# Two attention stages of one kernel: where the causal mask is added, and which PSUM banks hold the scores

## The reference

```
# layer 0, cut to what matters (x: 16 x 256 x 256)
q, k, v = rope(x1 @ w_qkv.T + b_qkv)          # x1: x after a cross attention with a side input
scores  = q @ k.T / sqrt(16)                  # 16 heads of 16 channels, 256 x 256 per head
scores  = where(causal, scores, -inf)
out     = softmax(scores) @ v @ w_out.T + b_out
x = x + out;  x = x + fp4_ffn(category_linear(x))

# layer 1
du      = reaction_diffusion(x)
q, k, v = rope(rms_norm(du) * g @ W_qkv)      # 16 heads of 64 channels
q, k, v = cut into two segments of 128 tokens each
k, v    = 16 memory keys / values put in front: 144 keys per segment
scores  = where((j < 16) | (j - 16 <= i), q @ k.T / 8, -1e30)
x = x + softmax(scores) @ v @ W_out;  x = x + mixture_of_experts(mlp(x))
```

## Time and profile before

| | before |
|---|---|
| median of three runs | 2669.96 us |
| the profiled execution, its span | 2665.8 us, 2664.1 us |
| PE busy | 2463.0 us (92%) |
| PEld busy | 2191.2 us (82%) |
| DVE busy | 1836.6 us (69%) |
| ACT busy | 1229.0 us (46%) |
| POOL busy | 939.4 us (35%) |
| mean granted TensorE clock | 0.957 of full |

### The profile page before, as it was taken

One profiled execution on the slowest core, in us unless ns is written; L12 is line 12 of the kernel. 1 busy time (PEld: TensorE's weight loads), 2 busy tenths in 40 slices (PEclk: granted clock), 3 DMA queues, 4 the chain that ended last, 5 costly groups with the idle time before them and its releaser, 6 DMA issues.

```text
span 2664.1 us, 55131 instructions
## 1 busy us (share of the span) xinstructions
PE 2463.0 (92%) x19904; PEld 2191.2 (82%) x19904; DVE 1836.6 (69%) x3887; ACT 1229.0 (46%) x3774; POOL 939.4 (35%) x1016
## 2 busy tenths in 40 slices
PE   4799999999998559999999999979999999999999
PEld 3578778778877447888888888769999999999999
DVE  5666766766766556656666656447876988888877
ACT  2455555555555124554545454433333565555522
POOL 4332432333332324444544444402332222222054
PEclk7899999999998779999999999989999999999999
DMA  3221121111111032222112221122113677777534
GB/s 112 88 54 33 43 54 33 43 47 41 43 23 28 0 108 47 48 52 51 43 44 51 52 48 44 46 53 72 41 41 110 223 231 233 228 240 229 183 98 129
DMA packets 153077, 225.74 MB, mean 85 GB/s; under 512 B 54294, under 2 KB 123174, under 8 KB 142054
## 3 DMA queue, kind: packets, MB, share of 16 engines
q1 hardware_dynamic: 143942, 203.56, 26.7%
q0 software_dynamic: 8864, 18.66, 2.7%
HBM read 159.32 MB, written 27.16 MB: 70 GB/s over the span
## 4 chain that ended last, share of the span: by engine, by line
PE 75%; DVE 10%; ACT 7%; issue 4%; DMA 1%; POOL 1%; SPq 0%; another core or an unknown queue 0%; ACTq 0%; POOLq 0%; DVEq 0%
PE bank L55 56%; PE bank L140 6%; PE bank L1155 3%; ACT P L1336 2%; PE bank L1193 2%; PE bank L319 2%; PE bank L315 2%; PE bank L344 1%; PE bank L1150 1%; DVE qm L826 1%; PE bank L308 1%; DVE qr L833 1%; ACT L1384 1%; PE bank L1188 1%; ACT PTh L604 1%
## 5 line engine op out<-in xcount | busy, mean ns | idle before, releaser
L1336 ACT ACTIVATE P<-bank,mx 128x144 f32<-128x144 f32 x512 | 188.3, 380 | 373.0 <-DVE mx L1434 373.0
L1021 POOL TENSOR_TENSOR xe<-xe 128x704 f32<-128x704 f32 (+3 forms) x64 | 86.5, 1351 | 501.2 <-DVE xe L846 499.9
L55 PE MATMUL bank<-xD_hi,w1e_lo 128*128 128x256 f32 x880 | 254.2, 289 | 0.0
L55 PE MATMUL bank<-xD_hi,w1e_hi 128*128 128x256 f32 x880 | 249.4, 283 | 0.0
L55 PE MATMUL bank<-xD_lo,w1e_hi 128*128 128x256 f32 x880 | 249.3, 283 | 0.0
L55 PE MATMUL bank<-w2e_hi,hrD_lo 128*128 128x256 f32 x880 | 249.0, 283 | 0.0
L55 PE MATMUL bank<-w2e_lo,hrD_hi 128*128 128x256 f32 x880 | 249.0, 283 | 0.0
L55 PE MATMUL bank<-w2e_hi,hrD_hi 128*128 128x256 f32 x880 | 249.0, 283 | 0.0
L592 ACT ACTIVATE Ph<-bank,mx 128x128 f32<-128x128 f32 x256 | 93.9, 367 | 322.1 <-DVE mx L738 278.3
L2358 POOL DMA_INDIRECT xE<-d_y,ixs x78 | 110.9, 1422 | 343.4 <-PE bank L140 316.4
L1991 ACT ACTIVATE hD<-bank,b1E 128x256 f32<-128x256 f32 x312 | 128.6, 473 | 199.2 <-PE bank L55 191.8
(11 more groups left out here) (320 smaller groups left out, 7994.6 us busy)
## 6 DMA issues: line engine op xcount, KB each, us to landing
w1raw<-in_ew SPq DMA_DIRECT2D x39, 1024.0 KB, 5.8
w2raw<-in_ew SPq DMA_DIRECT2D x39, 1024.0 KB, 5.0
K<-Kn SPq DMA_DIRECT2D x256, 72.0 KB, 2.1
d_ys<-oE SPq DMA_DIRECT2D x39, 256.0 KB, 2.4
d_rot<-QK SPq DMA_DIRECT2D x16, 512.0 KB, 4.0
Rs<-d_rot SPq DMA_DIRECT2D x64, 128.0 KB, 4.3
Q<-Qn SPq DMA_DIRECT2D x128, 64.0 KB, 2.0
later<-Qn SPq DMA_DIRECT2D x128, 64.0 KB, 2.0
```

The source lines that it names most:

```text
L55: inst = e.matmul(out, l, r, start=k == 0, stop=k == len(pairs) - 1)
L1021: e.tensor_tensor(x, x, s, ALU.add).then_inc(*po.up())
L1336: inst = e.activation(P1[t % 2][:, n, :], bank[:, 144 * sg:144 * sg + 144], ACT.Exp, bias=mx1[t % 2][:, 2 * g + sg:2 * g + sg + 1], scale=1.0,
```

## The change

There are four edits.

1. The mask products on PE go, with `identb`. The mask is now added by DVE inside the pass that takes the maximum: `tensor_tensor_reduce` writes -(score + mask) to `Ph` (stage c: `P1`) in SBUF, and its accumulator gives the minimum of that, which is the negated maximum. Each such call is two instructions on DVE, one that streams and one that writes the accumulator out. There are four calls in a step of either stage; in stage c they take the place of two instructions.
2. ACT computes the exponential in place in SBUF, with scale -1.
3. Scores always use banks 0 and 1, turned weights banks 2 and 3. `scores(P+1)` therefore waits for `maxima(P)` (`v_mx`), and the wait for the copies of the pair before (`c_PT`) moves to `turn_heads`. In stage ab the three score blocks of a head become two products, of 128 and 256 columns.
4. In step 1 of stage ab ACT runs `spread_copy(b-1)` ahead of `exps(P+1)`, no longer behind it.

```diff
         def mask(n):
-            return maskb[:, 144 - n:144].rearrange("p (o n) -> p o n", o=1).broadcast_to((128, 2, n))
+            return maskb[:, 256 - n:256]
...
             # pe_ab, scores(P)
-                bank = [banks[2 * (P % 2) + g] for g in range(2)]
-                for g in range(2):
-                    if P >= 2:
-                        e.wait_ge(c_PT, 2 * P - 3 + g)
-                    e.matmul(bank[g][:, 0:384].rearrange("p (a n) -> p a n", a=3)[:, 0:3:2, :], identb, mask(128),
-                             start=True, stop=False)
+                bank = banks[0:2]
+                if P:
+                    e.wait_ge(v_mx, 2 * P)
...
-                for g in range(2):
-                    e.matmul(bank[g][:, 0:128], q[g][:, 0:128], k[g][:, 0:128], start=False, stop=False)
-                for c in range(2):
-                    at = slice(128 * c, 128 * c + 128)
+                for st in range(2):
                     for g in range(2):
-                        inst = e.matmul(bank[g][:, 128 + 128 * c:256 + 128 * c], q[g][:, 128:256], k[g][:, at],
-                                        start=False, stop=c == 1)
+                        inst = e.matmul(bank[g][:, 128 * st:128 + 256 * st], q[g][:, 128 * st:128 * st + 128],
+                                        k[g][:, 0:128 * st + 128], start=True, stop=True)
             # turn_heads(P)
                     e.wait_ge(c_P, 2 * P + g + 1)
-                    turn(e, [(banks[2 * (P % 2) + g][:, c * 128:c * 128 + 128], Ph[P % 2][g][:, c, :])
+                    if P:
+                        e.wait_ge(c_PT, 2 * P - 1 + g)
+                    turn(e, [(banks[2 + g][:, c * 128:c * 128 + 128], Ph[P % 2][g][:, c, :])
...
             # act_ab, exps(P)
-                    if P >= 2:
-                        e.wait_ge(p_T, 2 * (P - 2) + g + 1)
-                    e.activation(dst[:, 0, :], bank[:, 0:128], ACT.Exp, bias=mx[:, 0, n:n + 1], scale=1.0,
+                    e.activation(dst[:, 0, :], dst[:, 0, :], ACT.Exp, bias=mx[:, 0, n:n + 1], scale=-1.0,
...
             # act_ab, the loop
+                    if p == 1:
+                        spread_copy(b - 1)
                     exps(P + 1)
                     if p == 0:
                         x1_high(b + 1)
-                    if p == 1:
-                        spread_copy(b - 1)
...
             # dve_ab, maxima(P)
-                    e.tensor_reduce(mx[:, 0, n:n + 1], bank[:, 0:128], AX.X, ALU.max, negate=True)
-                    e.tensor_reduce(mx[:, 1, n:n + 1], bank[:, 128:384], AX.X, ALU.max, negate=True).then_inc(v_mx, 1)
+                    bank, dst = banks[g], Ph[P % 2][g]
+                    if P >= 2:
+                        e.wait_ge(p_T, 2 * (P - 2) + g + 1)
+                    for st in range(2):
+                        inst = e.tensor_tensor_reduce(
+                            dst[:, st:2 * st + 1, :], bank[:, 128 * st:128 + 256 * st].rearrange("p (a n) -> p a n", n=128),
+                            mask(128 + 128 * st).rearrange("p (a n) -> p a n", n=128),
+                            -1.0, 1e30, ALU.add, ALU.min, mx[:, st, n:n + 1])
+                    inst.then_inc(v_mx, 1)
...
             # pe_c, scores(t)
-                if t >= 2:
-                    e.wait_ge(c_PT1, 2 * t - 2)
-                    e.wait_ge(v_PT1, t - 1)
-                for g in range(2):
-                    e.matmul(bank[g][:, 0:288].rearrange("p (o n) -> p o n", o=2), identb, mask(144), start=True, stop=False)
+                if t:
+                    e.wait_ge(v_mx1, 2 * t)
...
             # dve_c, maxima(t)
                 if t >= 2:
+                    e.wait_ge(p_T1, 2 * t - 2)
                     e.wait_ge(c_P1, t - 1)
                 for g in range(2):
-                    e.tensor_reduce(mx1[t % 2][:, 2 * g:2 * g + 2],
-                                    banks[2 * (t % 2) + g][:, 0:288].rearrange("p (a n) -> p a n", a=2),
-                                    AX.X, ALU.max, negate=True).then_inc(v_mx1, 1)
+                    for sg in range(2):
+                        inst = e.tensor_tensor_reduce(
+                            P1[t % 2][:, 2 * sg + g, :], banks[g][:, 144 * sg:144 * sg + 144], mask(144),
+                            -1.0, 1e30, ALU.add, ALU.min, mx1[t % 2][:, 2 * g + sg:2 * g + sg + 1])
+                    inst.then_inc(v_mx1, 1)
```

More of the change, by code:

```diff
@@ L603, in copy_turned @@
                         e.wait_ge(p_PV, P // 2 - 1)
-                    e.activation(PTh[P // 2 % 2][2 * (P % 2) + g], banks[2 * (P % 2) + g][:, 0:384], ACT.Copy
+                    e.activation(PTh[P // 2 % 2][2 * (P % 2) + g], banks[2 + g][:, 0:384], ACT.Copy
                                  ).then_inc(c_PT, 1)
@@ L1162, in turn_heads @@
                     return
-                P = P1[t % 2]
-                bank = [banks[2 * (t % 2) + g] for g in range(2)]
+                P, bank = P1[t % 2], banks[2:4]
                 e.wait_ge(g_n1, t + 1)
+                if t:
+                    e.wait_ge(c_PT1, 2 * t)
                 outs = [(bank[0][:, 128 * sg:128 * sg + 128], P[:, 2 * sg, 16:144]) for sg in range(2)]
@@ L1343, in copy_turned @@
                     return
-                bank = banks[2 * (t % 2)]
+                bank = banks[2]
                 e.wait_ge(p_T1, 2 * t + 1)
```

29 lines of the change are left out of this document (11 added, 18 removed).

## The result

| kernel | median of the runs, us | lowest to highest | profiled execution, us | its span, us |
|---|---|---|---|---|
| before | 2671.07 (4 runs) | 2663.75 to 2673.55 | 2665.8 | 2664.1 |
| changed | 2626.57 (4 runs) | 2625.69 to 2638.05 | 2638.05 | 2636.3 |

The ratio is 0.9848, with a 95% interval from 0.9814 to 0.9881: 44.5 us less, where 20 were forecast. The profiled execution of the changed kernel is the longest of its four, at a mean granted clock of 0.948; the other three had 0.956 to 0.960. So the two traces show only 27.8 of the 44.5 us, and the rest has to be explained too.

What follows compares the result with a forecast made beforehand. PE bounds the kernel, with DVE close behind. Stage ab -9 us, its clock +7, stage c -22 and the stage ends +3 make -21 us: 2650 us against the median of before, range 2595 to 2700 (8 in 10).

Steps and rivals of the forecast that it cites:

- The four masks of the sum: Stage ab, steps 2 to 4 and 5 to 7, set by PE: four mask steps of 0.31 us fall away, -1.24 us a batch.
- DVE's write-out: Accumulator write of each new DVE call: 0.08 us each, so 0.32 us more a step in stage ab.
- Rival A: Slower: DVE becomes the bound, write-outs cost 0.20 us and stage c's clock falls each batch; 2701 us, chance 0.22.
- ACT: Exponentials read SBUF instead of PSUM: 0.02 us more on each of four, 0.08 us a step.
- Stage ab's batch: All four stretches of a stage ab batch, clock left out: -0.60 us, times 15 batches -9 us.
- the two stretches that DVE sets: Stage ab, scores of step 7 to second `project` and scores of step 4 to `down`: each +0.32 us a batch.
- The clock term: Stage ab: two PE waits a batch should each bring a stretch at half clock; +0.5 us a batch, +7 us in all.
- My sum: Whole kernel: -9 + 7 - 22 + 3 = -21 us, then set against the median of before, 4.2 us above its profiled execution.
- total of 20: Stage c some 20 us shorter; its batches were put at -1.5 us each, times 15: -22 us.
- the path to the turn: Stage c, scores to turn through maxima, exponentials, ACT, DVE and POOL: +0.2 us a batch, with PE waiting 1.2 us there.
- Rival C: No change: as forecast, but stage c's 1.2 us wait brings half clock each batch, +22 us; 2672 us, chance 0.22.
- Rival B: Much faster: waits don't come back, stage c gains 46 us and stage ab's clock stays up; 2585 us, chance 0.14.

Runs made afterwards that it cites:

- ab_only: The change in stage ab alone, stage c as in the kernel before; ratio to before 0.9989.
- before_fill: The kernel before with five useless products on PE ahead of the mask products of step 5 in stage ab; ratio to before 0.9956.
- after_again: The changed kernel once more, unaltered, in other rounds on another chip; 2679.7 us, ratio to before 0.9907.
- fill: The changed kernel with eight useless products on PE ahead of `down` in step 5 of stage ab; 2658.0 us, ratio to before 0.9845.
- no_mask: The kernel before without its mask products and nothing in their place, so future positions stay unmasked; ratio to before 0.9941.
- copy_back: The changed kernel with the copy of the spread sums put back behind the four exponentials of its step; 2645.7 us, ratio to before 0.9898.

## Why the prediction was right, and where it was off

**Direction, place and most of the path were right.** Stage c was to be "some 20 shorter": 20.3 in the first pair of traces, and it took 783.8 to 786.9 us in the eight more traces that have all of the change there. With the form of before it took 805.25, and 808.5 and 809.9 in `ab_only` and `before_fill`, with the same batches and other ends, so 20 to 25 us by the pair that one takes. Stage ab was to be "as long as before within 5 us": -3.3 in `after_again`, but -7.7 in the first trace, outside of it. In stage ab the waits came where they were named: none for `PTh`, 2.25 us at `down` (forecast 2.6), 2.06 us in front of the second `project` (forecast some 3). In stage c the wait of about 1 us for POOL's `Pm` in one step of eight did not come.

**Masks:** in stage ab PE's busy time fell by the 2.51 us of eight mask steps at 0.31, but where PE sets the time a step gives back only 0.24. The four masks of the sum brought 0.94, not 1.24. In stage c eight of them took 1.64 us off PE's busy time, not 2.8.

**DVE's write-out:** the duration was right (0.08), the step from it to the sum was wrong. I added it to the queue; it runs beside the next instruction. A set costs 0.05 more in stage ab (forecast 0.32), 0.18 in stage c (0.48). Rival A fell with it. **ACT** was off the other way: 0.16 a step, not 0.08. Together 0.21 where 0.40 was forecast in stage ab. In stage c the exponentials of a step take 1.61 us for 1.44, 0.17 more; together 0.35 against 0.56.

**Stage ab's batch** without its clock: -0.73 measured, -0.60 forecast. That these are so near is partly luck, for two sizes were off in opposite ways: the masks brought 0.30 less than forecast, and the two stretches that DVE sets grew by 0.18 instead of 0.64, since DVE and ACT got 0.19 us a step less than I had counted.

**The clock term** was mis-sized too, and moved the total most. I took +0.5 us a batch as a fixed price. The runs show two cases. Full clock would give 48.41. Where the half clock recurs in every batch (10.2 us of it, an estimate from the mean of 0.90) the batch takes 51.20, so the clock costs 2.79; in the five full batches ahead of that in the first trace it is 50.48 on average, 2.07. The kernel before pays 51.25 less 49.14, 2.11. So the term is 0 or +0.7, by execution. I had let two waits bring a stretch each, both at a price; two stretches came, but the one ahead of the second `project` is free and the one behind `down` costs all of the 2.8. The profiled execution lies 11.5 us above the median of all four; seven of its batches had the second case, which makes 5 of it. By the executions of `ab_only`, where 0.021 of mean clock went with 28.9 us, the 0.008 to 0.012 more of the other three would be 11 to 17 us (9 to 13 by a line through all twelve). They weren't profiled, so this is an argument and not shown.

**The whole 44.5** then: 20.3 from stage c, 7.7 from stage ab in the trace, 11.5 from the other executions' clock (by this reading), and 5.3 since the profiled execution of before was that much below its median, less 0.2 in stage d. My sum added 4.2 for the last and nothing for the third.

**Stage c's** total of 20 was near by luck: its errors cancelled. A batch brought 1.06 us (47.92 less 46.86), not 1.5. PE's idle time grew by 0.58 us, less than forecast, and the path to the turn got 0.23 us shorter, not 0.2 longer; but its busy time fell by only 1.64. Why a mask step is worth only 0.2 us of busy time there is open. The ends brought the other 4 us (beyond fifteen batches the stage has 82.1 us left for 86.4), where I let them cost.

**Rival C** (half clock in stage c): its clock stayed at 1.00. **Rival B** (clock up, waits gone) fell on the waits; `fill` shows that its clock half was possible, and worth some 22 us against `after_again`.

**Open:** why executions of one kernel fall into the repeating pattern in some rounds and not in others; why the changed kernel's batch of 48.41 us, with the same wait of 2.25 us, had no stretch at half clock; and why kernels with different work (`no_mask`, `copy_back`, `ab_only`) settle at the same 51.20 us. The last means that two such kernels can't be compared by their settled batches.

## What to carry to other kernels

When PE waits a microsecond or two in every turn of a loop, look at the granted clock behind the wait before you price the change: batches of the same instructions differed by 2.8 us here, nearly four times what the change of this stage was worth. Compare loop turns at the same clock, one by one, and only then the totals. And price an instruction by the start of the next one, not by its own duration, and its removal by what its two neighbours gain on each other.

## What the runs showed of the hardware

- A wait of 2.25 us on PE was followed by some 6.8 us at the 1.2 GHz level in each batch (443.60:450.40, clock 0.51); with products of no use in the wait the clock of the batch was 1.00. A kernel that did more work was 22 us faster than `after_again`, in other rounds. A wait of 2.25 us is not enough by itself: the batch of 48.41 us had it too, at a clock of 1.00.
- What half clock cost in the changed kernel depended on where it fell: some 6.8 us of it behind `down` made that stretch 2.8 us longer, some 3.4 us of it ahead of the second `project` added nothing (19.70 us with and without, `after_again` and the first trace).
- The stretches at half clock can repeat from batch to batch, all of 51.20 us within 0.1, in four different kernels (`ab_only`, `after_again`, and later in the stage `copy_back` and `no_mask`), and the executions of one kernel lie up to 29 us (`ab_only`) and 22 us (`after_again`) apart.
- DVE's accumulator write-out (0.08 us) started with the next instruction, a one-column write (0.06 us) 0.03 us behind its start, and they add 0 to 0.01 us each to the queue.
- A fused add and minimum that also writes its sum took as long as a plain reduction of its width: 283 and 416 ns on average for 128 and 256 columns, against 282 (L737) and 412 ns.
